# A linear-attention and expert kernel on one core: the key path placed ahead of the query path, epsilon as an extra key column

## The reference

```
x = x + ln(attn_block(ln(x)))        # random-feature attention and a feed-forward product
x = x + ln(moe_block(ln(x)))         # 8 experts, each takes its 512 best tokens

attn_block(video):
  q, k, v = heads(video @ Wq.T + bq), heads(video @ Wk.T + bk), heads(video @ Wv.T + bv)   # 16 heads of 16
  qp = exp(q' @ proj.T - |q|^2/8 - max over the 64 features)       + EPS_K
  kp = exp(k' @ proj.T - |k|^2/8 - max over features and tokens)   + EPS_K
  out = (qp @ (kp.T @ v)) / (qp @ sum over tokens of kp)
  x = ln(video + out @ Wo.T + bo) * g2 + be2
  return ln(x + relu(x @ W1.T + b1) @ W2.T + b2) * g3 + be3

moe_block(x):
  scores = softmax(x @ gate.T); for each expert the top 512 tokens, ln, fc1, gelu, fc2, times the score, added to x
```

## Time and profile before

| | us |
|---|---|
| median of 3 runs (lowest to highest) | 788.98 (788.41 to 790.06) |
| the profiled execution | 789.41 |
| its span, first to last instruction | 787.70 |
| PE busy | 724.5 (92%) |
| DVE busy | 619.9 (79%) |
| ACT busy | 469.8 (60%) |
| POOL busy | 377.1 (48%) |

### The profile page before, as it was taken

One profiled execution on the slowest core, in us unless ns is written; L12 is line 12 of the kernel. 1 busy time (PEld: TensorE's weight loads), 2 busy tenths in 40 slices (PEclk: granted clock), 3 DMA queues, 4 the chain that ended last, 5 costly groups with the idle time before them and its releaser, 6 DMA issues. The chain is left out here.

```text
span 787.7 us, 16101 instructions
## 1 busy us (share of the span) xinstructions
PE 724.5 (92%) x5948; PEld 592.8 (75%) x5948; DVE 619.9 (79%) x1307; ACT 469.8 (60%) x749; POOL 377.1 (48%) x358
## 2 busy tenths in 40 slices
PE   8999999999999999999999979875899999999950
PEld 7867768778778778778678668765788889998850
DVE  5876678888888888888898797888857777677683
ACT  4656747867867767868857835464245544455470
POOL 4364317527527527617616613511437576554563
PEclk9899999999999999999999999999699999999985
DMA  8100010011011011011011021250346664456593
GB/s 250 34 2 2 1 54 2 27 54 57 28 53 54 27 53 54 27 53 54 27 54 30 32 71 35 62 190 1 93 161 170 154 158 105 115 152 167 130 270 115
DMA packets 51184, 62.60 MB, mean 79 GB/s; under 512 B 9408, under 2 KB 44992, under 8 KB 51136
## 3 DMA queue, kind: packets, MB, share of 16 engines
q1 hardware_dynamic: 44016, 49.74, 19.5%
q0 software_dynamic: 6864, 12.19, 7.9%
q10 hardware_dynamic: 256, 0.03, 0.0%
HBM read 40.85 MB, written 21.10 MB: 79 GB/s over the span
## 5 line engine op out<-in xcount | busy, mean ns | idle before, releaser
L2166 PE MATMUL pF<-w,h 128*128 128x256 f32 x448 | 109.8, 386 | 0.0
L2166 PEld LDWEIGHTS pF<-w,h 128*128 128x128 f32 x448 | 80.7, 190 | 17.6 <-issue 8.6
L1131 POOL DMA_INDIRECT kp<-row_scratch,idx_g x32 | 43.2, 1350 | 73.5 <-DVE idx_g L1838 49.7
L896 ACT ACTIVATE h<-pX,b1cur 128x512 f32<-128x512 f32 x64 | 44.0, 689 | 53.8 <-DVE b1cur L1938 39.4
L2618 PE MATMUL pX<-w_lo,h_hi 128*128 128x256 f32 x256 | 73.9, 289 | 0.8 <-issue 0.8
L985 POOL TENSOR_SCALAR ve<-mv 128x4 f32<-128x4 f32 x36 | 8.5, 236 | 134.4 <-DVE mv L1208 133.4
L2618 PE MATMUL pX<-w_hi,h_lo 128*128 128x256 f32 x256 | 72.4, 283 | 0.0
L2618 PE MATMUL pX<-w_hi,h_hi 128*128 128x256 f32 x256 | 72.4, 283 | 0.0
L1139 POOL DMA_INDIRECT acc_scratch<-qp,idx_s x28 | 58.0, 2073 | 22.3 <-DVE qp L1875 17.4
L1896 DVE TENSOR_TENSOR h_lo<-h,h_hi 128x512 fp32r<-128x512 f32 x64 | 42.7, 690 | 24.6 <-ACT h_hi L888 24.6
L1313 DVE RECIPROCAL den<-den 128x512 f32<-128x512 f32 x14 | 46.9, 3348 | 7.9 <-ACT den L544 7.9
(11 more groups left out here) (434 smaller groups left out, 2157.9 us busy)
## 6 DMA issues: line engine op xcount, KB each, us to landing
kp<-fc1T SPq DMA_DIRECT2D x8, 1024.0 KB, 7.2
w<-fc2T SPq DMA_DIRECT2D x8, 1024.0 KB, 8.2
xin<-video SPq DMA_DIRECT2D x7, 512.0 KB, 3.7
x<-video SPq DMA_DIRECT2D x7, 512.0 KB, 4.4
out<-x SPq DMA_DIRECT2D x7, 512.0 KB, 3.0
acc_scratch<-xf SPq DMA_DIRECT2D x7, 512.0 KB, 2.9
row_scratch<-y SPq DMA_DIRECT2D x7, 512.0 KB, 3.0
kp<-acc_scratch SPq DMA_DIRECT2D x4, 512.0 KB, 5.3
```

The lines of the kernel that those rows point to most:

```text
L896: nc.scalar.activation(h[:, n, :], pM[n % M_SLOTS], ACT.Gelu_apprx_tanh, bias=b1cur[:, n:n + 1]).then_inc(he_ready, 1)
L1131: pool.indirect_dma_start(xg[:, g, :], None, row_d, bass.IndirectOffsetOnAxis(ap=idx_g[:, g:g + 1], axis=0)).then_inc(gathered, 16)
L2166: ins = nc.tensor.matmul(pF[m][:, half * D:(half + 1) * D], h[:, k, tok(2 * m + half)], w2[:, k, :], start=(k == 0), stop=(k == FC - 1))
```

## The change

- kp is stored as 8 pairs of 130 columns for 128 (`kpe`); the last two hold EPS_K. `context` multiplies 129 columns, so its last column is EPS_K times the sum of v; `cs_copy(i, 0)` on ACT copies that column to `vsum` and adds it to the context as a bias, and `cs_copy(i, 1)` adds N * EPS_K to the sums of keys. `eps_k` on ACT and the epsilon products of batch 0 on PE go, and two POOL passes that made `vsum` there.
- PE: `key_features(0)` stands ahead of `values`; the eight `hidden` products are placed otherwise among features; `context` stands ahead of `turn_tops`; `features_turned(1)` behind `sums_of_keys`; 16 of the 32 `ff_out` units for 22 stand ahead of `all_heads`.
- ACT: the key exponentials lie among the relus, z's second norm behind them, and the rows `y` at the very end.
- DVE: both first `k_max` ahead of `x2T_lo`; all four `k_sub` in a row, then `q_max` 2 and 3, the tops' parts and `qsq_lo`; scores and residual later; z's first norm is gone.
- POOL: norms z in four TENSOR_SCALARs (`z_normed`), adds x2's bias ahead of root 3, waits for all `k_sub` ahead of the sums of keys, and makes `xnb` last.
- SP: each batch's scores are stored one batch later, those of batch 6 behind the first expert's weight loads.

```diff
+PW = P + 2
...
-        kp = sb("kp", [P, TT, H * M])
+        kpe = sb("kp", [P, TT, PAIRS, PW])
+        kp = kpe[:, :, :, 0:P]
...
+                if not (isinstance(u, int) and u == 0):
+                    scores_out(u - 1)
+
+            def scores_out(u):
+
+                sp.wait_ge(sc_ready, u + 1)
+                sp.dma_start(row_t[u][:, :, D:ROW], sct[:]).then_inc(sc_out, 16)
...
             sp.wait_ge(f_ready, F_Z[1] + 1)
             load_expert(0)
+            scores_out(L2)
...
-                nc.scalar.activation(cs[:, n, :], pA[n][:, 0:G * P], ACT.Copy).then_inc(cs_ready, 1)
+                if n:
+                    nc.scalar.activation(cs[:, 1, :], pA[1][:, 0:G * P], ACT.Identity, bias=epsn_c[:, 0:1]).then_inc(cs_ready, 1)
+                else:
+                    wide = pA[0][:, 0:G * PW].rearrange("p (g x) -> p g x", x=PW)
+                    nc.scalar.activation(vsum[:].unsqueeze(2), wide[:, :, P:P + 1], ACT.Copy).then_inc(vsum_ready, 1)
+                    act.wait_ge(vsum_ready, i + 1)
+                    for g in range(G):
+                        ins = nc.scalar.activation(cs[:, 0, g * P:(g + 1) * P], wide[:, g, 0:P], ACT.Identity, bias=vsum[:, g:g + 1])
+                    ins.then_inc(cs_ready, 1)
 
             def exp_k(i, t):
 
                 act.wait_ge(ks_ready, i * TT + t + 1)
-                nc.scalar.activation(kp[:, t, :], kp[:, t, :], ACT.Exp).then_inc(kp_ready if is_first(i) else ke_ready, 1)
-
-            def eps_k(i, t):
-                act.wait_ge(ke_ready, (i - 1) * TT + t + 1)
-                nc.scalar.activation(kp[:, t, :], kp[:, t, :], ACT.Identity, bias=epsk_c[:, 0:1]).then_inc(kp_ready, 1)
+                nc.scalar.activation(kp[:, t], kp[:, t], ACT.Exp).then_inc(kp_ready, 1)
...
+                key_rows(1)
+                relu(f, 0)
+                relu(f, 1)
+                q_squares(i)
+                for n in range(2, 6):
+                    relu(f, n)
+                exp_k(i, 0)
+                relu(f, 6)
+                exp_k(i, 1)
+                relu(f, 7)
+                exp_k(i, 2)
+                exp_k(i, 3)
+                if ut:
+                    for t in range(3):
+                        z_norm(u, t)
+                q_tops(i)
+                if ut:
+                    z_norm(u, 3)
+                cs_copy(i, 0)
+                exp_q(i, 0)
+                cs_copy(i, 1)
+                exp_q(i, 1)
+                dens(i)
+                x_norm(i + 1)
+                heads_top(i, 0)
+                heads_top(i, 1)
+                xT_copy(i + 1)
+                    normed_rows(u)
...
+            def z_normed(u):
+
+                pool.wait_ge(rstd_ready[2], u + 1)
+                settled(pool)
+                for t in range(TT):
+                    ins = nc.gpsimd.tensor_scalar(z[:, t, :], z[:, t, :], mv[2][:, t, 0:1], rstd[2][:, t:t + 1], ALU.subtract, ALU.mult)
+                ins.then_inc(zn_ready, 1)
...
+                    z_normed(u)
                     z_affine(u)
                 if f is not None:
 
                     pool.wait_ge(f_ready, f * F_JOBS + J_X2T + 2)
                     nc.gpsimd.tensor_tensor(x2[:], x2[:], g2_b[:].unsqueeze(1).to_broadcast([P, TT, D]), ALU.mult).then_inc(x2b_ready, 1)
+                if f is not None:
+                    pool.wait_ge(x2b_ready, 2 * f + 1)
+                    nc.gpsimd.tensor_tensor(x2[:], x2[:], b2_b[:].unsqueeze(1).to_broadcast([P, TT, D]), ALU.add).then_inc(x2b_ready, 1)
                 if u is not None:
                     root(3, u)
                     shift(3, u, nz)
...
+                def biased_rows():
+
                     wait(pool, r_ready, i * 2)
                     pool.wait_ge(xn_ready, (i + 1) * TT)
                     nc.gpsimd.tensor_tensor(xnb[:], xn[:], bo_b[:].unsqueeze(1).to_broadcast([P, TT, D]), ALU.add).then_inc(xnb_ready, 1)
 
-                    for t in range(1, 1 if is_first(i) else TT):
+                if is_first(i):
+                    pool.wait_ge(bias_ready, 1)
+                    biased_rows()
+                else:
+                    pool.wait_ge(ks_ready, (i + 1) * TT)
+                    for t in range(1, TT):
                         pool.wait_ge(kp_ready, i * TT + t + 1)
                         if t > 1:
                             pool.wait_ge(ksum_ready, i * (TT - 1) + t - 1)
-                        nc.gpsimd.tensor_tensor(ksum, kp[:, 0, :] if t == 1 else ksum, kp[:, t, :], ALU.add).then_inc(ksum_ready, 1)
+                        nc.gpsimd.tensor_tensor(ksum_s, kp[:, 0] if t == 1 else ksum_s, kp[:, t], ALU.add).then_inc(ksum_ready, 1)
...
+                if not is_first(i):
+                    biased_rows()
...
+                k_top(i, sa)
+                q_max(i, 0)
+                q_max(i, 1)
+                dve.wait_ge(dg_ready, (i + 1) * 2)
+                k_shift(i)
+                for t in range(TT):
+                    k_sub(i, t)
+                q_max(i, 2)
+                q_max(i, 3)
+                parts_of_tops(i)
+                rest_of_squares(i)
+                if more:
+                    ln1_stats(i + 1)
+                if u is not None and not (isinstance(u, int) and u == 0):
+                    scores(u - 1)
+                heads_of_context(i)
+                sums_of_context(i, sa)
+                add_ff(0)
...
-                                ins = nc.tensor.matmul(s[32 * q:32 * q + 32, g * P:(g + 1) * P], v_[:, 32 * pair:32 * pair + 32],
-                                                       eps if k_ is None else k_[:, tok(place_of(pair))], start=(t == 0),
-                                                       stop=(t == len(steps) - 1), tile_position=(0, 32 * q))
+                                ins = nc.tensor.matmul(s[32 * q:32 * q + 32, g * PW:g * PW + P + 1], v[:, t, 32 * pair:32 * pair + 32],
+                                                       kpe[:, t, place_of(pair), 0:P + 1], start=(t == 0), stop=(t == TT - 1),
+                                                       tile_position=(0, 32 * q))
                     ins.then_inc(a_ready, 1)
...
+                key_features(1)
+                pe.wait_ge(x2l_ready, (f + 1) * C)
+                if is_ahead(i):
+                    pe.wait_ge(w1_split, C + 2)
+                hidden(0)
+                hidden(1)
+                pe.wait_ge(qT_ready, (i + 1) * G)
+                features(i, J_XQ, qT, 0)
+                hidden(2)
+                turn_kmax()
+                hidden(3)
+                hidden(4)
+                spread_kmax()
+                hidden(5)
+                features(i, J_XQ + 1, qT, 1)
+                hidden(6)
+                hidden(7)
+                ff_out(6)
+                context()
+                turn_tops()
+                ff_out(2)
+                features_turned(0)
+                ff_out(2)
+                sums_of_keys()
+                ff_out(2)
+                features_turned(1)
+                turn_context()
+                ff_out(4)
+                all_heads()
+                ff_out(5)
+                ff_out(3)
+                ff_out(3)
+                    ff_out(5)
+                turn_x(i + 1)
+                ff_out(5)
+                attention_out()
```

More of the change, by code:

```diff
@@ L719, in body @@
                     queries(i, 1)
+                    key_rows(0)
                     values(i, 0)
                     values(i, 1)
[L722 to L728 removed]
+                for c in range(C):
+                    take_f(f, J_X2T + c, x2T_hi[:, c, :], ACT.Copy, x2T_ready)
@@ L1428, in body @@
                     normed(1, f, x2, r).then_inc(x2_ready, 1)
-                if u is not None and not (isinstance(u, int) and u == 0):
-                    scores(u - 1)
-                if i is not None:
-                    sa = Steps(dve, dve_a, STEPS_A, i)
-                if u is not None:
-                    normed(2, u, z, z).then_inc(zn_ready, 1)
-                if is_ahead(i):
-                    k_max(i, 0)
-                if f is not None:
-                    for c in range(C):
-                        dve.wait_ge(x2T_ready, f * C + c + 1)
-                        nc.vector.tensor_tensor(x2T_lo[:, c, :], pF[c][:], x2T_hi[:, c, :].bitcast(F32), ALU.subtract).then_inc(x2l_ready, 1)
-                if i is not None:
-                    if not is_ahead(i):
-                        k_max(i, 0)
-                    k_max(i, 1)
-                    norms(i, 0, dgk)
-                    norms(i, 1, dgk)
+                sa = Steps(dve, dve_a, STEPS_A, i)
+                k_max(i, 0)
+                k_max(i, 1)
+                for c in range(C):
+                    dve.wait_ge(x2T_ready, f * C + c + 1)
+                    nc.vector.tensor_tensor(x2T_lo[:, c, :], pF[c][:], x2T_hi[:, c, :].bitcast(F32), ALU.subtract).then_inc(x2l_ready, 1)
+                norms(i, 0, dgk)
+                norms(i, 1, dgk)
+                k_max(i, 2)
```

(35 more changed lines are left out.)

183 lines of the change are left out of this document (32 added, 151 removed).

## The result

The changed kernel takes 793.64 us in the median of four runs (793.21 to 793.71), the kernel before 788.69 (787.89 to 790.06) beside it: a ratio of 1.0061, 95% interval 1.004 to 1.0082. It is 0.6% slower. The prediction said 788.5 us; its range, 785.5 to 797, holds the result; its forecast, 787 to 790 and for the most part no measurable change, does not.

The account below looks back on a forecast made before the run. TensorE itself was taken as the bound from the third batch on. Minus 0.9 (first batch), minus 0.2 (second) and plus 0.6 (shared port) made minus 0.5, 788.5 us for the median; 8-in-10 range 785.5 to 797.

Parts of the forecast that it names:

- the wait at 113.63: Second batch: PE's wait of 1.03 us goes, as the products by heads come six feed-forward units earlier; minus 1.0.
- The late store of the scores: End: seventh batch's scores stored behind the first expert's two weight loads; cost 0, at most 1.5 us.
- the handover: Shared port at 29.55, end of POOL's first sum of keys: nearly a tie, DVE taken to be first.
- If DVE is first, both its passes are through at 30.9: Shared port, batches three to eight: tops' rest and qsq_lo pass before POOL's next sum; sums of keys end at 35.7.
- the charge of 0.1 a batch: Batches three to eight: PE wants the sums of keys at 35.6, they end at 35.7; plus 0.6 in six batches.
- rival 3: POOL wins the port twice, qsq_lo waits for a third sum, turned features lose 3 us a batch: 806; chance 0.07.
- rival 2: POOL wins the port at 29.55, turn_tops 1.0 to 1.35 late in each of six batches: 795; 0.25 with rival 4.
- Every change between products by row groups and whole ones costs about 0.1 us: PE's own work, batches three to eight: one more at spread_kmax, one less at the context; 0, plus or minus 0.1 a batch.
- The z norm: POOL's four TENSOR_SCALARs of 128x256, taken as 3.2 us, with 2.9 and 5 kept as bounds.
- The end: After the last batch: eight units between gates and output product as before, so 0.
- rival 4: Long z norm (5 us): spread_kmax and the feature product lose 0.8 to 1.3 a batch, 794 to 797; 0.25 with rival 2.
- rival 1: PE loses nothing in the loop: minus 0.9, minus 1.0, minus 0.6 of switches, 786.5 us; chance 0.30.

Follow-up runs that it names:

- sum_waits: Changed kernel, but GpSimd's second and third sums of the keys wait until the rest of the squares (qsq_lo) is written; 795.47 us, ratio 1.0066.
- ordered: Changed kernel with qsq_lo directly behind the fourth k_sub and GpSimd's second sum of the keys waiting for the tops' rest; 792.16 us, ratio 1.0039.
- pe_spread: Changed kernel with TensorE's second query features directly behind the spread of the keys' maximum, hidden block 5 behind both; 797.01 us, ratio 1.0083.
- ordered_pe: ordered plus the move of pe_spread and, in the second batch, the second k_max behind x2T_lo; 791.77 us, ratio 1.0029.
- all_fixes: ordered_pe and znorm_dve together, on the changed kernel; 786.43 us, ratio 0.9975.
- znorm_dve: Changed kernel with the norm of z back on VectorE, behind the norm of x2, in place of GpSimd; 793.83 us, ratio 1.0054.
- eps_only: Kernel before with only the epsilon edits (129th column, biases of the copies, no eps_k), every order of work as before; 797.34 us, ratio 1.0109.

## Why the prediction was wrong

**What held.** TensorE is the bound, and work taken off ScalarE gave nothing in the loop. The first batch is 0.91 us shorter (forecast 0.9), both profiles having the same low clock in it. In the second batch x2T_lo is waited for 1.25 us against 0.47 (forecast 0.8 later), and the wait at 113.63 is gone (forecast 1.0):

```profile
71.90 0.50 PE L2099 MATMUL pF<-x2T_hi,w_lo 128*128 128x512 f32 x1 [1.25 <-DVE x2T_lo L1443]
```

The second batch is longer by 0.30 all the same, where the forecast had 0.2 less: the turned features wait 0.46 for the rest of the squares there too, and the prediction charged the port only from the third batch on. The late store of the scores cost nothing: it is not on the chain that ended last. VectorE did come first at the handover in every batch from the second on but the fourth.

**First failed step: "If DVE is first, both its passes are through at 30.9", and the charge of 0.1 a batch.** Behind the cast come two passes of two SBUF tiles, and I let the second through because it stands directly behind the first. It starts 0.14 us after it, and that is where GpSimd's second sum went in. qsq_lo took 3.24, which the prediction had named as the sign of rival 3; but it waited for one sum, not two, and TensorE comes to the turned features at 33.2, not at the forecast's 32.7, so that of some 2 us of delay it paid 0.45. sum_waits and ordered show it: with the port free, the first turned features start at 33.18 to 33.20 in place of 33.65. The fourth batch is the prediction's rival 2 (tops 0.74 late), the third its sdiag beside a pass of GpSimd (2.23).

**Second failed step: "Every change between products by row groups and whole ones costs about 0.1 us; there is one more [...] and one less [...] I take 0".** The price of one change is right, what the new order costs was not: the first half of the batch grew by 0.41 to 0.43. Little of it comes from the key features. TensorE starts the first hidden product behind both groups of them 12.64 us into the batch, with 48 products of 512 columns to start from there; before, 15.40 us into it, with 36. Twelve such products take 2.80 (0.233 each), so the key features cost 0.04. The other 0.39 arises behind that point, where the spread and the second query features, neighbours before, now stand apart. pe_spread and ordered_pe put them side by side again and got 0.08 to 0.14 back, with the features waiting for VectorE's second q_max. In all_fixes, where it ends sooner, 0.29 is back (the first feed-forward product at 26.87 for 27.16 in ordered). The last 0.1 is not tried: in these runs the features stand behind the spread, in the kernel before ahead of it. The second half, whose pieces were put in another order too, gave 0.20 back (58.32 less 27.17 against 58.08 less 26.73); which of the moves did it is open.

So a batch of the loop: 0.43 for the order, less 0.20, and 0.45 for the port make 0.68 of the 0.69 measured, where I had 0.1. **The z norm** was mis-sized as well (4.86 us, taken as 3.2, with 5 as a bound), but znorm_dve shows that in the changed kernel it cost only the third batch 0.5. That is luck: the diagonal (312.22 in the row above) comes where one of GpSimd's passes ends (312.44), and in the third batch it does not. **The end** was put at 0, but the eighth batch is 0.87 longer, as its output product waits 1.79 for VectorE's aT_lo (before 0.92); ordered, with the same wait, takes 0.51 of it back.

That the range holds the result is luck in part. Its upper end stood for rivals 2 and 4, with 0.25 between them, and neither took the time: rival 2 came in one batch of six, rival 4 in none of the loop. The lower end is also further out than the terms allow: without the waits and with 0.6 less of switches they make minus 2.5, as in rival 1, not minus 2.6 to minus 3.2.

The Trainium skill (SBUF — State Buffer, "SBUF: two separate sides") says that the pair of ports is locked for a whole instruction, by whoever starts first, and counts VectorE's fast modes, such as a float32 copy within SBUF, among the ones that need it. The trace agrees on both: a cast of 128x64 took 1.15 and 1.65 us beside a sum. The prediction cited the rule for passes with two inputs only, though its working let the cast wait as well. The Trainium skill (TensorEngine Tiling (Array Packing), "Key Properties") says that a change of the tiling mode drains the engine; the traces have 0.1 us more between the starts at each such change (0.33 in place of 0.23), which agrees.

## What to carry to other kernels

Where two engines share a port, the order of their passes has to be fixed by a semaphore; if it is left to a tie, a move that shifts arrivals by tenths of a us elsewhere can cost more than it gives (pe_spread: 0.27 a batch), and a pass taken out can cost 1.3 (eps_only). Work that seems a waste (here eps_k) may be what keeps a long pass of the other engine behind a short critical one: before it is removed, ask what starts sooner. And price a small product by its neighbours in the new order, one place at a time: the spread apart from the features cost 0.3 more than beside them.

## What the runs showed of the hardware

**The clock moves the time by 1 to 3 us.** The profiled executions differ in it. In the first batch, between 30 and 40 us, the granted clock was 0.66 on average in some executions and 0.83 or 1.00 in others, of kernels that do the same there; the batch took 41.25 to 41.27 us with 0.66 and 40.10 to 40.12 with the others (42.17 in the kernel before, with 0.66). Changed kernel, then eps_only:

```profile
30.00:40.00 10.00, 9.36 (x65) 9.01 (x58) 9.30 (x14) 4.60 (x7) 0.00 (x0) 0.66 0.16 53
```

```profile
30.00:40.00 10.00, 7.87 (x70) 7.02 (x74) 9.54 (x12) 5.40 (x7) 0.00 (x0) 1.00 0.17 55
```

The first expert starts at half clock (1.2 GHz) too. In sum_waits, ordered and ordered_pe the granted clock from 545 to 585 us was 0.70 on average, in the changed kernel and the kernel before 0.79, and from the experts' first turn to TensorE's end it took 198.4 to 198.6 us in place of 196.4 to 196.5. Whether that follows from the kernel or is chance was not tried.

**VectorE holds up GpSimd as well.** During four k_sub in a row GpSimd's power of 128x4 took 1.95 us, against 1.04, and the product of 128x4 behind it (L993) 1.02 against 0.20. VectorE's passes are 1.16 apart, so it looks as if GpSimd gets in between two of them; no run tried it alone.

**A TENSOR_SCALAR with two column operands** on 128x256 takes 1.2 us on GpSimd (4.86 for four) and 0.34 on VectorE (1.38 for four, in the kernel before), where GpSimd's plain one of 128x1024 takes 2.85.
